# Layer norms shared between two engines: every second token tile normalised by ScalarE

## The reference

```python
def _layernorm(x, axis=-1, eps=1e-05):
    m = jnp.mean(x, axis=axis, keepdims=True)
    v = jnp.var(x, axis=axis, keepdims=True)
    return (x - m) / jnp.sqrt(v + eps)
...
    h = _layernorm(x, axis=-1) * (1 + ca) + sa
    x = x + ga * _L0_attn_ref(h, ...)
    h = _layernorm(x, axis=-1) * (1 + cb) + sb
    x = x + gb * _L0_ffn_ref(h, ...)
```

## Time and profile before

| | |
|---|---|
| median of 3 runs | 2004.24 us (2002.46 to 2007.24) |
| profiled execution | 2012.43 us, span of its instructions 2010.6 us |
| busy, PE / DVE / ACT / POOL | 1231.8 / 1347.0 / 830.0 / 280.6 us |
| mean granted clock of PE | 0.772 of full |
| instructions | 28556 |

### The profile page before, as it was taken

How to read it: one execution, slowest core, us unless ns; L and a number is a source line. 1 busy time by engine, 2 the same in 40 slices (tenths; PEclk the granted TensorE clock), 3 DMA queues, 4 the chain that set the end, 5 groups by cost and what they waited for, 6 DMA issues and landing times. The chain is left out here.

```text
span 2010.6 us, 28556 instructions
## 1 busy us (share of the span) xinstructions
PE 1231.8 (61%) x10381; PEld 609.3 (30%) x10382; DVE 1347.0 (67%) x2969; ACT 830.0 (41%) x1538; POOL 280.6 (14%) x271
## 2 busy tenths in 40 slices
PE   6689999999999994659741630403045877621144
PEld 4122222222222223559530410201023545520033
DVE  4799999899999905364443248586877676577711
ACT  3068888889888993122100320300022354410021
POOL 3100000000000000123014340100044300100033
PEclk9579999999999996679955865756566968755567
DMA  2301111111111000000052310000014132110012
GB/s 61 43 6 27 24 18 18 24 25 20 18 24 26 3 2 13 17 0 1 1 159 75 104 32 0 0 0 0 0 34 105 21 36 34 43 47 1 0 48 58
DMA packets 50679, 58.87 MB, mean 29 GB/s; under 512 B 11832, under 2 KB 39483, under 8 KB 50268
## 3 DMA queue, kind: packets, MB, share of 16 engines
q1 hardware_dynamic: 45579, 49.78, 12.1%
q0 software_dynamic: 4224, 6.01, 1.2%
q10 hardware_dynamic: 736, 1.25, 0.2%
HBM read 30.17 MB, written 13.63 MB: 22 GB/s over the span
## 5 line engine op out<-in xcount | busy, mean ns | idle before, releaser
L609 ACT ACTIVATE l0att_probs<-l0att_ps_sv 128x512 f32<-128x512 f32 x1024 | 555.6, 595 | 129.6 <-PE l0att_ps_sv L581 120.3
L637 DVE TENSOR_REDUCE l0att_half_negmax<-l0att_ps_m 128x1 f32<-128x1024 f32 x480 | 551.3, 1215 | 39.5 <-PE l0att_ps_m L525 39.5
L550 PE MATMUL l0att_ps_sv<-l0att_probs,l_V_aug 128*32 128x256 f32 x4096 | 340.5, 399 | 0.0
L581 PE MATMUL l0att_ps_sv<-l_Q,l_K 51*128 51x512 bf16 x1024 | 204.8, 397 | 22.5 <-ACT l0att_probs L609 20.4
L525 PE MATMUL l0att_ps_m<-l_K,l_Q 48*128 48x512 bf16 x960 | 190.0, 393 | 19.2 <-DVE l0att_half_negmax L637 14.7
L550 PEld LDWEIGHTS l0att_ps_sv<-l0att_probs,l_V_aug 128*32 128x32 f32 x4096 | 89.7, 108 | 186.9 <-issue 110.1
L581 PEld LDWEIGHTS l0att_ps_sv<-l_Q,l_K 51*128 51x128 bf16 x1024 | 49.3, 93 | 244.4 <-ACT l0att_probs L609 232.4
L257 PE MATMUL ada_ps<-ident_sb,xn 128*128 128x128 f32 x128 | 34.3, 459 | 139.3 <-DVE xn L250 139.3
L311 POOL CAST l0att_nm<-l0att_negmax 128x16 bf16<-128x16 f32 x16 | 3.1, 197 | 559.8 <-DVE l0att_negmax L622 559.8
L2384 ACT ACTIVATE l3loc_probs<-l3loc_ps_s 128x320 f32<-128x320 f32 x128 | 49.0, 435 | 57.7 <-PE l3loc_ps_s L2363 57.1
L2570 PE MATMUL l3sel_ps_c<-l3sel_part,l3sel_ones 128*128 128x15 bf16 x56 | 10.9, 194 | 99.3 <-DVE l3sel_part L2595 99.3
(11 more groups left out here) (565 smaller groups left out, 2312.2 us busy)
## 6 DMA issues: line engine op xcount, KB each, us to landing
l_Q<-l_qp SPq DMA_DIRECT2D x188, 32.0 KB
l_K<-l_kp SPq DMA_DIRECT2D x188, 32.0 KB
l3f_mlp_l_w<-in_l_w_dram SPq DMA_DIRECT2D x2, 2048.0 KB
l_sorted_in<-l1ffn_zeros SPq DMA_DIRECT2D x1, 3072.0 KB
l1exp_rows<-l_sorted_in SPq DMA_DIRECT2D x4, 768.0 KB, 4.8
l_sorted_out<-l1exp_y SPq DMA_DIRECT2D x4, 768.0 KB, 5.6
l_Q<-l_q_parts SPq DMA_DIRECT2D x18, 128.0 KB
l_K<-l_k_parts SPq DMA_DIRECT2D x18, 128.0 KB
```

Of the source, the lines that this page charges most:

```text
L550: mm = pe.matmul(ps_v[32 * c:32 * c + 32, cols], V_aug[:, kt, h, :], probs[:, kt % 2, c, cols], start=(kt == 0 and part == 0), stop=(kt == ...
L581: pe.matmul(ps_s[:, (n + i) % 3, :], K[at, h % HEAD_BUFS, c1(kt)], Q[at, h % HEAD_BUFS, c4(2 * pair + i)], start=True, stop=True).then_inc ...
L609: act.activation(probs[:, kt % 2, c, :], ps_s[:, n % 3, :], ACT.Exp).then_inc(expd, 1)
L637: dve.tensor_reduce(half_negmax[:, h % 2, t, half:half + 1], src, AX_X, ALU.max, negate=True).then_inc(m_read, 1)
```

## The change

The even tiles are normalised by VectorE as before, the odd ones by ScalarE. ScalarE's operation computes scale * x + bias, so it needs an offset -mean * rstd per token; VectorE forms it for all 16 tiles in one instruction after `rstd`. ScalarE's list puts the odd tiles between the evictions. In the calls with a transpose its order is: tiles 1, 3, 5, eviction 0, tiles 7, 9, eviction 1, tiles 11, 13, eviction 2, tile 15, eviction 3. TensorE still transposes the tiles in the order 0 to 15 and waits for each from its own engine. In the calls without a transpose, ScalarE normalises its eight tiles in a row.

```diff
+        offset = st.sb("offset", [P, NT])
...
-        tile_normed = st.sem("tile_normed")
+        even_normed = st.sem("even_normed")
+        odd_normed = st.sem("odd_normed")
+        offset_ready = st.sem("offset_ready")
...
                 link(dve.tensor_tensor(rstd[:], rstd[:], corr[:], ALU.mult))
-                for t in range(NT):
+                dve.scalar_tensor_tensor(offset[:], mv[:, :, 0], -1.0, rstd[:], ALU.mult, ALU.mult)\
+                   .then_inc(offset_ready, 1)
+                for t in range(0, NT, 2):
                     dve.tensor_scalar(normed[:, t, :], src[:, t, :], mv[:, t, 0:1], rstd[:, t:t + 1],
-                                      ALU.subtract, ALU.mult).then_inc(tile_normed, 1)
+                                      ALU.subtract, ALU.mult).then_inc(even_normed, 1)
...
                 for t in range(NT if turned is not None else 0):
-                    pe.wait_ge(tile_normed, t + 1)
+                    pe.wait_ge(odd_normed if t % 2 else even_normed, t // 2 + 1)
...
                 act.activation(std[:], var[:], ACT.Sqrt).then_inc(std_ready, 1)
-                for j in range(NC4 if turned is not None else 0):
-                    act.wait_ge(bank_full, j + 1)
-                    act.activation(turned[:, c4(j)], ps[:, j, :], ACT.Identity, bias=shift_col, scale=scale_col)
+                act.wait_ge(offset_ready, 1)
+                for t in range(1, NT + 2, 2):
+                    if t < NT:
+                        act.activation(normed[:, t, :], src[:, t, :], ACT.Identity, bias=offset[:, t:t + 1],
+                                       scale=rstd[:, t:t + 1]).then_inc(odd_normed, 1)
+                    if turned is not None and t >= 5 and t % 4 == 1:
+                        j = t // 4 - 1
+                        act.wait_ge(bank_full, j + 1)
+                        act.activation(turned[:, c4(j)], ps[:, j, :], ACT.Identity, bias=shift_col, scale=scale_col)
```

## The result

The changed kernel took 2032.43 us (median of 4 runs, 2027.09 to 2035.83), the kernel before 2005.67 (median of 4). The ratio is 1.0133, with a 95% interval of 1.0106 to 1.0160: 27 us slower, between 21 and 32. 2027.0 had been forecast, with a range of 2013 to 2037. A second comparison, with other runs of both kernels, gave 1.0144 (1.0113 to 1.0176).

The account below looks back on a forecast made before the run. VectorE's normalising pace was taken to bound the norm stages, though by little. The terms 21.9 - 1.6 + 3 gave +23 us on the median of 2004.24, so 2027 us, range 2013 to 2037.

Parts of the forecast that it names:

- the relay: Norm stage: VectorE normalises, TensorE transposes, ScalarE evicts; VectorE sets the pace at 0.257 us a tile, the last eviction ends it.
- Part 1: VectorE in each norm stage: one added offset product of 0.23 us, eight tiles fewer, done at about T+2.3.
- Part 2: ScalarE: one normalised tile takes 0.47 us (bounds 0.33 and 0.56) and occupies the engine for 0.38 us.
- Part 3: Ten stages with a transpose: tiles queued behind evictions lengthen each by 2.19 us, +21.9 us in all (+15 to +27).
- The closed loop: Stages with a transpose: eviction, tile and transpose follow one another once per bank, 1.72 us against 1.03 before.
- Part 4: The two stages without a transpose: ScalarE's eight tiles end at T+3.40 instead of 4.19, together -1.6 us.
- The bound of -3.9: Largest gain for the two stages without a transpose, if VectorE's 2.3 us ends last.
- the low end: Whole kernel: +9 us, 2013, from ten stages at +1.5, the plain ones at -3.9 and a clock gain of 2.
- Part 5: TensorE's clock behind the norms rises later: 1.9 us for each of three blocks, 0 to +5.8, taken as +3 us.
- the bounds of the loop: Stages with a transpose: 1.49 to 1.90 us per bank, +1.5 to +2.7 a stage, +15 to +27 for ten.
- The first two rivals: Norm stages: ScalarE keeps up, about -7.6 us, 1997; or overlap shortens the rounds, no visible change, about 2004; chance 0.04 each.
- The third: Blocks behind the norms: the lower clock stays in force more widely, +11 in place of +3, 2036; chance 0.08.

Follow-up runs that it names:

- the warm changed kernel: The changed kernel plus 28 identity transposes on TensorE in each of the twelve norm stages, ahead of its wait for the first tile; 1.0183 to the kernel before.
- The kernel with tiles first: The changed kernel, but ScalarE normalises all eight of its tiles before its first eviction; 1.0087 to the kernel before.
- the one with 2.2 us ahead of the tiles: The kernel before plus eleven repeated statistics on VectorE ahead of the tiles in the ten norms with a transpose; 1.0162 to the kernel before.

## Why the prediction was right

**What bounds a stage** (the relay, VectorE's pace, the last eviction): right. Kernels with fewer tiles on VectorE and no loop ran at TensorE's 3.73 us for sixteen transposes, as the bound of 0.22 a tile said.

**Part 1.** The offset took 0.175 us instead of 0.23, and VectorE went on 0.09 after its start. It was done 2.1 us after its first tile. Nothing hung on it.

**Part 2.** A tile took 482 ns, 473 had been worked out. Eight in a row spanned 3.19 us, 0.387 apart, against 0.38.

**Part 3.** The closed loop is right in kind and size: 1.72 us per bank measured, 1.72 forecast, +2.11 to +2.27 us a stage against 2.19. With the tiles taken out from behind the evictions it falls to +0.5 to +0.7, which shows that the order is the cause.

**Part 4.** -0.80 and -0.81, against -0.79 each. The bound of -3.9 comes out at -3.8 by its own terms (2 x (4.19 - 2.3)), which moves the low end by nothing that counts.

**Part 5.** This is the term that was mis-sized. Its premise held: the thinner transposes leave the lower clock in force, and none, or one, of the ten blocks behind opened at 2.4 GHz. The size, +3 us, was too small. Measured beyond the stages were 7 us in the first comparison and 9 in the second (intervals from 1 to 12 and from 3 to 15), above the 5.8 that had been named as the most. Two steps made it small. It took the four blocks of one trace as all that could be lost, while other traces of kernels with the stages nearly as before show five or six. And it left out l3norm, whose eight-column matmuls were held to be indifferent to the clock: they took 6.97 us instead of 5.04. That the total still fell within the range is owed to the room that the bounds of the loop left; the loop itself came out within 0.3 us of its forecast.

The twelve traces together show where the lower clock was paid for. The block behind the norm that opens layer 2 took 87.8 to 88.1 us in the five traces in which it opened at 0.9 or more, and 89.7 to 91.1 in the seven others. Behind l2norm1 it was 162.9 to 163.4 (five) and 164.1 to 166.6 (seven), behind l3norm 229.5 to 230.4 (five) and 230.7 to 232.7 (seven). Behind the norm that opens layer 1 it was 147.4 to 147.9 in five traces and 148.9 to 151.0 in seven, one of which had opened high. These four blocks together took 630.8 us on average in the six traces of kernels whose stages are no more than 0.3 us longer than before (628.6 to 634.2), and 636.4 and 635.0 in the two of the changed kernel: 4 to 6 us. The blocks behind the first norm and behind the one that opens layer 3, which the prediction had counted, vary by 10 to 11 us whatever the clock was at their start, and show no price.

By the Trainium skill, "TensorE: Matmul & The Clock Gate", section "HAM oscillation — how this bites in real kernels", a matmul kernel whose bursts are parted by waits for transfers is throttled again in each wait. Those waits are longer than the pauses here; the warm changed kernel shows the clock going from 1.00 to 0.50 within the norm with pauses of 0.58 to 0.76 us between the clusters of transposes.

**The sum.** 20.0 in the stages and some 8 beyond, against 20.3 + 3. The first two rivals are out: ScalarE does not keep up, and the loop isn't cut short. The third, the clock in full, gave 2036 for +11; the measured excess lies between it and the forecast, and 2032.43 nearer to it.

**What stays open.** The kernel with tiles first and the one with 2.2 us ahead of the tiles also have an excess, 7 us or more and 4 us or more by their intervals. With tiles first, the four blocks named above took 637.5 us, 7 more than on average, and only one of them had opened at 0.9 or more; so there too much of the excess is in them. With 2.2 us ahead of the tiles they took 632.9, 2 more, and where the rest of that excess lies isn't settled. The traces are of one execution each, and single blocks of one and the same program differ by up to 8 us between traces. For the changed kernel the lost clock is shown in the traces and accounts for 4 to 6 us; that it makes up the whole excess is not shown.

## What to carry to other kernels

When an idle engine is given work, write down its list in order and ask of each new item what it stands behind: here an engine with over half its time free became the bound, since each tile that fed the next eviction was queued behind the last one, and a round trip of eviction, tile and transpose took the place of a pipeline. Work for an engine of that kind goes ahead of its first wait, or the waiting work goes to another engine. And a chain with gaps on TensorE has a second price, which falls in the blocks behind it; a single trace is too few to size it by.

## What the runs showed of the hardware

Thinning a burst can lower TensorE's clock while the burst is still running: in the warm changed kernel it was granted 1.00, then 0.80, then 0.50 over six microseconds in which TensorE was busy for 3.1.

A busy TensorE can lose it too: in the kernel before, behind l3norm, it was counted as busy all the time, with eight-column matmuls, while the clock went from 1.00 to 0.53. The rows are length, busy PE, PEld; clock; DMA:

```profile
1780.88:1782.88 2.00, 2.00 (x19) 2.00 (x19) 1.00 0.00 0
1782.88:1784.88 2.00, 2.00 (x12) 2.00 (x12) 0.53 0.00 0
```

Warming it ahead of time gave nothing: 28 extra transposes in each of twelve stages (1.0021, from 0.9997 to 1.0044).

The start of the program varies without any change to it. The first norm began at 24.76 us in the trace of before and at 29.56 in the second trace of the changed kernel. In the latter, TensorE's matmuls of the setup block stayed at their slow pace for longer (12 one-column matmuls in 2.56 us at 17.76, where before they took 1.69 us at 17.70):

```profile
17.70 1.69 PE L153 MATMUL setup_ps_c<-setup_silu,setup_wmod 128*128 128x1 f32 x12
```

```profile
17.76 2.56 PE L153 MATMUL setup_ps_c<-setup_silu,setup_wmod 128*128 128x1 f32 x12
```

The column of the granted clock shows 1.00 there in both, so in that block the durations are the better witness.
